# A two-layer network on one core: the feed-forward weights are quantised in five wide pieces between the first tiles' steps

## Chip, cores and metric

One core of a Trainium2 chip runs the whole network in one launch. The metric is the device time in microseconds (us); of several executions the median counts. The engines are named TensorE (PE, with its weight loads PEld), VectorE (DVE), ScalarE (ACT), Pool (GpSimd) and SP, which here only issues DMAs.

## The reference, cut to what matters

The network has two layers over 8 batches of 1024 tokens of width 256: attention and a feed-forward block, then two Mamba layers and a second feed-forward block. Each block's input is normalised and modulated, and its output is scaled by a gate and added to what came in. The change is in the feed-forward block, which is called twice with other weights:

```python
def fp4_quant_dequant(x):
    xb = x.reshape(shape[:-1] + (shape[-1] // 16, 16))
    scale = jnp.maximum(jnp.max(jnp.abs(xb), axis=-1, keepdims=True) / 6.0, 1e-12)
    idx = jnp.searchsorted(_MID, jnp.abs(xb / scale))
    return (_GRID[idx] * jnp.sign(xb / scale) * scale).reshape(shape)

def fp4_linear(x, w):
    return jnp.einsum('bsk,nk->bsn', fp4_quant_dequant(x), fp4_quant_dequant(w))

gate = fp4_linear(x, w_gate)        # w_gate, w_up: 704 x 256, w_down: 256 x 704
h = jax.nn.silu(gate) * fp4_linear(x, w_up)
x = x_in + gb * fp4_linear(h, w_down)      # x is layernorm(x_in) * (1 + cb) + sb
```

Weights and activations are both quantised along their rows, in groups of 16, to a 4-bit grid.

## The kernel before

The phases run one after the other. Each phase is a block of five programs, one for an engine, that hand over by semaphores; between blocks stand two barriers of all engines, with the clearing of the semaphores between them. The two feed-forward calls (`ffn_phase`) are the sixth part and the last part of the program.

In `ffn_phase` the weights come first, in a block of their own, `turn_weights`. It has 14 jobs: six slices of `w_gate` of 128 rows (the last has 64) by 256 columns, six of `w_up`, and two of `w_down` of 128 rows by 704 columns. SP loads a slice, VectorE quantises it in place with ten instructions (`fp4_round`, then `fp4_scale`), TensorE transposes it by chunks of 128 columns (L203), and ScalarE copies each chunk from PSUM into `wg`, `wu` or `wd` (L214). All buffers but the temporary ones are double.

Then a second block works through 64 tiles of 128 tokens. Its five programs are in step by `run`, which calls a `body` for n = -4, -3, ... and in it works on tiles at up to seven stages at once: `early` (statistics of tile n+4, on VectorE and Pool), `ahead` (ScalarE centres tile n+3, L1600; Pool multiplies and adds the modulation, L1414 and L1420), `norm` (quantising the input of tile n+2: VectorE L1469 to L1530, ScalarE L1604, Pool's scale L118), `turn` (tile n+1: TensorE transposes it, ScalarE copies it, TensorE multiplies it by `wg` and `wu`, L1578), `middle` (tile n: VectorE multiplies gate and up, L1476, and quantises the 704 columns of the result; ScalarE L1618, Pool L118), `hturn` and `last` (transposes and product with `wd`, L1548, gate and residual). So the first body that touches a weight is that of n = -1. The order of each engine's queue is that of the code, and an engine that waits for a semaphore runs nothing behind that wait. At the head of the block SP loads the modulation rows (`mod`, the same 24 KB into each of the 128 partitions); VectorE and Pool wait for it before anything else.

Of the kernel before, what the change touches and what calls it, by code (L numbers as in the profile page):

```python
# [10 lines left out]
U32 = mybir.dt.uint32  # L11
# [4 lines left out]
P = 128  # L16
# [1238 lines left out]
def ffn_phase(nc, name, x_in, x_out, mods, w_gate, w_up, w_down, ident, batches):  # L1255
# [7 lines left out]
    with ExitStack() as ctx:  # L1263
        def sb(n, shape, dt=FP32):
            return ctx.enter_context(nc.sbuf_tensor(f"{name}_{n}", shape, dt))
# [10 lines left out]
        wd = sb("wd", [P, FC, D])  # L1276
        jobs = []
        for w, t in ((w_gate, wg), (w_up, wu)):
            for r in range(0, FFN, P):
                n = min(P, FFN - r)  # L1280
                jobs.append((w[r:r + n, :], "fp4", [t[:, c, r:r + n] for c in range(DC)]))
        for r in range(0, D, P):
            jobs.append((w_down[r:r + P, :], "fp4",
                         [wd[0:min(P, FFN - c * P), c, r:r + P] for c in range(FC)]))
        turn_weights(nc, f"{name}_w", ident, jobs)

        mod = sb("mod", [P, batches, 3, D])
        x = sb("x", [P, 2, D])
# [24 lines left out]
        out_ps = pb("out_ps", [P, BANK])  # L1313

        s_mod, s_half = sem("mod_loaded"), sem("half_set")
        s_x = [sem(f"x_loaded{i}") for i in range(2)]
# [9 lines left out]
        s_xstep, s_hstep = sem("xstep_done"), sem("hstep_done")  # L1326
        s_store = [sem(f"stored{i}") for i in range(2)]
        QSTEPS, AT_MASK = 7, 5
        TIGHT = 1.0 + 2.0 ** -22
# [8 lines left out]

        def run(eng, body):


            for n in range(-4, 4):
                body(Tile(n // 2, n % 2), *stages(n))
            with eng.Fori(2, tiles // 2 - 2) as j:
                for u in range(2):
                    body(Tile(j, u), *stages(4))
            for n in range(tiles - 4, tiles + 2):
                body(Tile(n // 2, n % 2), *stages(n))
# [9 lines left out]
        def _(sp):  # L1358
            sp.dma_start(mod[:, :, :, :].rearrange("p b k d -> p b (k d)"), mods.rearrange("b k d -> b (k d)")
                         .unsqueeze(0).to_broadcast([P, batches, 3 * D])).then_inc(s_mod, 16)  # L1360

# [13 lines left out]
            load_x(Tile(0, 1))  # L1375
            load_xr(Tile(0, 0))
            for t in range(2, 6):
                load_x(Tile(t // 2, t % 2))
# [20 lines left out]
        def _(pool):  # L1399
            pool.memset(magic[:, :], MAGIC).then_inc(s_magic, 1)  # L1400
            pool.memset(half[:, :], -0.5).then_inc(s_half, 1)
            pool.memset(eps[:, :], EPS).then_inc(s_half, 1)
            pool.wait_ge(s_mod, 16)
            pool.wait_ge(s_half, 2)

            def body(t, early, ahead, norm, turn, middle, hturn, last):
# [39 lines left out]
                if middle:  # L1446
# [3 lines left out]
                    fp4_scale(pool, hq[:, u, :], hscale[:, :], P, FFN).then_inc(s_hq, 1)  # L1450
            run(pool, body)

        @block.vector
        def _(dve):
            dve.wait_ge(s_mod, 16)
            v = nc.vector

            def blocks(a):
                return a.rearrange("p (n k) -> p n k", k=BLOCK)

            def body(t, early, ahead, norm, turn, middle, hturn, last):
# [69 lines left out]
                if middle:  # L1531
# [3 lines left out]
                    hstep.issued(v.tensor_tensor(hd, hd, htmp[:, :], ALU.subtract))  # L1535
            run(dve, body)

        @block.tensor
        def _(pe):
            def body(t, early, ahead, norm, turn, middle, hturn, last):  # L1540
                if last:
# [28 lines left out]
                if turn:  # L1570
# [4 lines left out]
                    for w, at in ((wg, 0), (wu, 2)):  # L1575
# [5 lines left out]
                        mm.then_inc(s_gate if at == 0 else s_gu, 1)  # L1581
            run(pe, body)

        @block.scalar
        def _(act):
            act.wait_ge(s_magic, 1)

            def body(t, early, ahead, norm, turn, middle, hturn, last):
# [31 lines left out]
                if turn:  # L1620
# [5 lines left out]
                                         gu_ps[:, 0:2, 0:HALF], ACT.Silu).then_inc(s_silu, 1)  # L1626
            run(act, body)

# [765 lines left out]
```

## Time and profile before

| | us |
|---|---|
| median of three executions | 9688.74 |
| the other two | 9687.07, 17838.1 |
| the profiled execution, its own time | 9684.03 |
| its span, first to last instruction | 9682.3 |
| VectorE busy | 8401.1 (87%) |
| TensorE busy, mean granted clock | 8268.4 (85%), 0.939 |
| ScalarE, Pool busy | 5602.5 (58%), 4998.8 (52%) |

All stages and durations below are from the profiled execution, whose span starts at 0. A busy share over the whole program says little here, since it is a mean over phases that have different limits; the stages around the change must be looked at by themselves.

### The profile page before, as it was taken

What the parts mean: (1) busy time and instruction counts of PE and PEld (TensorE: products, weight loads), DVE (VectorE), ACT (ScalarE), POOL (GpSimd) and SP (SyncE); (2) the same over time, 40 slices, a digit from 0 to 9 for tenths busy, and PEclk for the clock granted to TensorE, in tenths of its full rate; (3) what the DMA queues carried; (4) which work ended last, traced back from release to release, by engine and by line L of the source; (5) the groups of instructions that cost most, each with busy time, mean ns of one, the idle gap of its engine ahead of it and who ended that gap; (6) DMA issues with size and microseconds to landing.
All of it is one profiled execution on the core that took longest, in us unless ns stands there. A gap on an engine that the chain in (4) does not pass through costs nothing. (4 is left out here: it accounts for less than half of the span.)

```text
span 9682.3 us, 173958 instructions
## 1 busy us (share of the span) xinstructions
PE 8268.4 (85%) x48396; PEld 4738.3 (49%) x48396; DVE 8401.1 (87%) x13204; ACT 5602.5 (58%) x9153; POOL 4998.8 (52%) x4685
## 2 busy tenths in 40 slices
PE   5679999999999997599688888887688888888599
PEld 2356667666666665366233333333233333333366
DVE  4668888888888886799599999999599999999799
ACT  2257777777777774233466666665466656555233
POOL 0000000000000000388599999999599999999487
PEclk7789999999999998799899999999899999999799
DMA  6789888888888887211112222111122222221111
GB/s 191 252 266 284 278 283 282 282 282 282 282 280 282 280 284 224 71 42 42 72 66 78 80 80 80 72 55 75 63 78 86 89 89 89 89 75 65 46 42 41
DMA packets 1174163, 1447.35 MB, mean 149 GB/s; under 512 B 83658, under 2 KB 1053914, under 8 KB 1140992
## 3 DMA queue, kind: packets, MB, share of 16 engines
q1 hardware_dynamic: 1173824, 1444.18, 45.4%
q14 instruction: 291, 2.38, 0.1%
q8 instruction: 48, 0.79, 0.0%
HBM read 880.81 MB, written 564.60 MB: 149 GB/s over the span
## 5 line engine op out<-in xcount | busy, mean ns | idle before, releaser
L1964 POOL TENSOR_TENSOR mb_bx<-mb_dtu,mb_bc 128x512 f32<-128x512 f32 x2048 | 2665.2, 1325 | 7.7 <-DVE mb_hs L2064 7.4
L2207 PE MATMUL mb_y_ps<-mb_g,ident 128*128 128x512 f32 x4096 | 2189.0, 641 | 467.9 <-DVE mb_g L2024 238.1
L2251 ACT ACTIVATE mb_dA<-mb_dt,mb_a_neg 128x512 f32<-128x512 f32 x2048 | 1403.3, 689 | 1616.2 <-DVE mb_hs L2064 1080.0
L1400 POOL MEMSET f_magic<- 128x1 f32 x2 | 0.2, 99 | 3617.7 <-POOLq L127 3617.7
L2207 PEld LDWEIGHTS mb_y_ps<-mb_g,ident 128*128 128x128 f32 x4096 | 763.6, 199 | 1646.1 <-issue 726.1
L1011 ACT ACTIVATE at_tab<-at_e_ps 128x384 f32<-128x384 f32 x2064 | 1015.1, 492 | 774.9 <-PE at_e_ps L928 773.5
L1065 DVE TENSOR_REDUCE at_nmax<-at_s_ps 128x1 f32<-128x1024 f32 x1025 | 1255.4, 1225 | 35.2
L944 PE MATMUL at_pT_ps<-ident,at_probs 128*128 128x128 f32 x8192 | 1117.7, 279 | 102.5 <-ACT at_probs L1016 81.9
L1016 ACT ACTIVATE at_probs<-at_s_ps,at_nmax 128x1024 f32<-128x1024 f32 x1025 | 1142.9, 1115 | 60.4 <-DVE at_nmax L1065 39.2
L944 PEld LDWEIGHTS at_pT_ps<-ident,at_probs 128*128 128x128 f32 x8192 | 894.3, 141 | 413.2 <-ACT at_probs L1016 384.9
L2024 DVE TENSOR_TENSOR mb_g<-mb_hs,mb_bc 128x512 f32<-128x512 f32 x1472 | 996.1, 677 | 33.8 <-PE mb_y_ps L2207 32.4
L2064 DVE TENSOR_TENSOR_SCAN mb_hs<-mb_dA,mb_carry,mb_bx 128x512 f32<-128x512 f32 x736 | 936.2, 1284 | 97.3 <-POOL mb_bx L1964 36.3
L2064 DVE TENSOR_TENSOR_SCAN mb_hs<-mb_dA,mb_bx 128x512 f32<-128x512 f32 x736 | 896.9, 1224 | 75.1 <-POOL mb_bx L1964 36.9
L911 PE MATMUL at_s_ps<-at_opnd 105*128 105x512 bf16 (+3 forms) x2818 | 805.0, 326 | 7.4 <-DMA at_skew<-at_tables 7.4
L1971 POOL TENSOR_TENSOR mb_g<-mb_hs_sb,mb_bc 128x512 f32<-128x512 f32 x576 | 750.9, 1304 | 88.3 <-PE mb_y_ps L2207 80.1
L1063 DVE TENSOR_TENSOR at_s_ps<-at_s_ps,at_skew 128x384 f32<-128x384 f32 (+1 forms) x1025 | 543.1, 530 | 272.5 <-PE at_s_ps L915 156.0
L1070 DVE COPY at_probsT<-at_pT_ps 128x512 f32<-128x512 f32 x1024 | 697.4, 681 | 0.0
L963 PE MATMUL at_c_ps<-at_probsT,at_val 128*32 128x128 f32 x16384 | 659.7, 279 | 1.6 <-ACT at_probsT L1023 1.6
L915 PE MATMUL at_s_ps<-ident,at_skew 128*128 128x128 f32 x2818 | 609.3, 274 | 0.0
L2140 PE MATMUL mb_ring<-mb_xc,mb_diag 128*128 128x512 f32 x1024 | 522.9, 596 | 48.2 <-ACT mb_u L2304 45.1
L963 PEld LDWEIGHTS at_c_ps<-at_probsT,at_val 128*32 128x32 f32 x16384 | 384.9, 109 | 211.9 <-issue 201.6
L915 PEld LDWEIGHTS at_s_ps<-ident,at_skew 128*128 128x128 f32 x2818 | 392.2, 142 | 85.0 <-issue 0.4
(236 smaller groups left out, 14151.9 us busy)
## 6 DMA issues: line engine op xcount, KB each, us to landing
at_tables<-at_tab SPq DMA_DIRECT2D x1032, 384.0 KB, 3.9
at_skew<-at_tables SPq DMA_DIRECT2D x1030, 256.0 KB, 3.1
mb_bc<-mb_bc_rows SPq DMA_DIRECT2D x256, 1024.0 KB, 6.4
at_skew<-at_tables SPq DMA_DIRECT2D x773, 128.0 KB, 3.5
at_opnd<-at_q_st SPq DMA_DIRECT2D x130, 210.0 KB, 4.4
at_opnd<-at_kl_st SPq DMA_DIRECT2D x130, 210.0 KB, 4.7
at_opnd<-at_kr_st SPq DMA_DIRECT2D x130, 210.0 KB, 4.7
at_q_st<-st_parts SPq DMA_DIRECT2D x96, 256.0 KB, 3.2
```

Source lines behind the costliest of these rows:

```text
L911: mm = nc.tensor.matmul(s_ps[:, b, a * P:z * P], opnd[:, u, 0, q], opnd[:, u, side, a * P:z * P], start=True, stop=(len(near) == 0))
L915: mm = nc.tensor.matmul(s_ps[:, b, kt * P:(kt + 1) * P], skew[:, u, 1, kt, blk * P:(blk + 1) * P], ident[:, :], start=False, stop=(kt == n ...
L944: mm = nc.tensor.transpose(pT_ps[:, hb, k * P:(k + 1) * P], probs[:, i % 2, c:c + P], ident[:, :])
L963: mm = nc.tensor.matmul(c_ps[lane * VW:(lane + 1) * VW, q:q + P], val[:, h.u, k + lane, :], probsT[:, i0 % 2, (k + lane) * P:(k + lane + 1 ...
L1011: nc.scalar.activation(tab[:, e, :], e_ps[:, 0:BAND], ACT.Copy).then_inc(s_tab, 1)
L1016: nc.scalar.activation(probs[:, i % 2, :], s_ps[:, i % 2, :], ACT.Exp, bias=nmax[:, i % 2:i % 2 + 1], scale=1.0).then_inc(s_exp, 1)
L1065: nc.vector.tensor_reduce(nmax[:, b:b + 1], s_ps[:, b, :], axis=AX.X, op=ALU.max, negate=True).then_inc(s_max, 1)
L1964: pool.tensor_tensor(bx[:, s % RINGS, :], dtu[:, c, :], bc[:, 0, n, :], ALU.mult).then_inc(s_bx, 1)
L2024: nc.vector.tensor_tensor(g[:, s1 % RINGS, :], state(s1), bc[:, 1, n, :], ALU.mult).then_inc(s_g, 1)
L2064: nc.vector.tensor_tensor_scan(state(s), dA[:, s % DA_RING, :], bx[:, s % RINGS, :], initial=carry[:, s:s + 1] if k.u else 0.0, op0=ALU.mu ...
L2207: nc.tensor.matmul(y_ps[:, c % 2, :], ident[:, :], g[:, s1 % RINGS, :], start=False, stop=(n == STATE - 1)).then_inc(s_y, 1)
L2251: nc.scalar.activation(dA[:, s % DA_RING, :], dt[:, c, :], ACT.Exp, scale=a_neg[:, c, n:n + 1]).then_inc(s_dA, 1)
```

## The change

The block `turn_weights` is gone from the feed-forward phase. The weights are now cut into five pieces, each a tile of 128 partitions: rows 0 to 127 and 128 to 255 of `w_down` (704 columns each), the first 640 rows of `w_gate` as five slices side by side (1280 columns), the same of `w_up` (1280), and the 64 remaining rows of both, one above the other (256). A function `prepare(k)` of each engine's program does one step: VectorE runs the front half of piece k (absolute maximum, stride, reciprocal, product, mask: five instructions) and the back half of piece k-1 (add, subtract). ScalarE makes the magic number between them, in place of a VectorE instruction, and Pool works out the scale and multiplies by it. TensorE transposes piece k-1 into `gu_ps`, the PSUM tile that holds gate and up later, and ScalarE copies the whole of it to `wg`, `wu` or `wd` in one or two instructions. `run` calls `prepare(0)` and `prepare(1)`, then `prepare(2)`, `(3)`, `(4)` and `(5)` each ahead of the bodies n = -4, -3, -2 and -1. TensorE doesn't start the body n = -1 before all five pieces have been copied. The load of `mod` is issued behind those of the weights and of the first tiles; VectorE waits for it in `prepare(5)`, Pool in `prepare(3)`.

```diff
--- before.py
+++ after.py
@@ -1274,16 +1274,28 @@
         wg = sb("wg", [P, DC, FFN])
         wu = sb("wu", [P, DC, FFN])
         wd = sb("wd", [P, FC, D])
-        jobs = []
-        for w, t in ((w_gate, wg), (w_up, wu)):
-            for r in range(0, FFN, P):
-                n = min(P, FFN - r)
-                jobs.append((w[r:r + n, :], "fp4", [t[:, c, r:r + n] for c in range(DC)]))
-        for r in range(0, D, P):
-            jobs.append((w_down[r:r + P, :], "fp4",
-                         [wd[0:min(P, FFN - c * P), c, r:r + P] for c in range(FC)]))
-        turn_weights(nc, f"{name}_w", ident, jobs)
-
+
+        edge = FFN // P * P
+        tail = FFN - edge
+        widths = (FFN, FFN, edge // P * D, edge // P * D, D)
+        starts = tuple(sum(widths[:k]) for k in range(len(widths)))
+        jobs = len(widths)
+        raw = sb("w_raw", [P, sum(widths)])
+        made = sb("w_made", [P, sum(widths)])
+        wtmp = sb("w_tmp", [P, sum(widths)])
+        wamax, wstride, winv, wscale = (sb(n, [P, sum(widths) // BLOCK]) for n in ("w_amax", "w_stride", "w_inv", "w_scale"))
+
+        def part(a, k):
+            return a[:, starts[k]:starts[k] + widths[k]]
+
+        def blocks_of(a):
+            return a.rearrange("p (n k) -> p n k", k=BLOCK)
+
+        def part_blocks(a, k):
+            return a[:, starts[k] // BLOCK:(starts[k] + widths[k]) // BLOCK]
+
+        def spread(a, k):
+            return part_blocks(a, k).unsqueeze(2).to_broadcast([P, widths[k] // BLOCK, BLOCK])
         mod = sb("mod", [P, batches, 3, D])
         x = sb("x", [P, 2, D])
         xr = sb("xr", [P, 2, D])
@@ -1312,6 +1324,8 @@
         hT_ps = pb("hT_ps", [P, 2 * BANK])
         out_ps = pb("out_ps", [P, BANK])
 
+        turned_up = gu_ps[:, :, :].rearrange("p (c a) w -> p c (a w)", c=DC)
+        turned_down = gu_ps[:, 0:2, :].rearrange("p a w -> p (a w)")
         s_mod, s_half = sem("mod_loaded"), sem("half_set")
         s_x = [sem(f"x_loaded{i}") for i in range(2)]
         s_xr = [sem(f"xr_loaded{i}") for i in range(2)]
@@ -1325,6 +1339,10 @@
         s_shift, s_magic = sem("shift_done"), sem("magic_set")
         s_xstep, s_hstep = sem("xstep_done"), sem("hstep_done")
         s_store = [sem(f"stored{i}") for i in range(2)]
+        s_raw = [sem(f"weights_loaded{k}") for k in range(jobs)]
+        s_wfront, s_wstep, s_wback, s_wscale = sem("wfront"), sem("wstep"), sem("wback"), sem("wscale")
+        s_wq, s_wT, s_wkept = sem("wq"), sem("wT"), sem("w_kept")
+        FRONT, BACK = 5, 2
         QSTEPS, AT_MASK = 7, 5
         TIGHT = 1.0 + 2.0 ** -22
         xt = x_in.rearrange("(n p) d -> n p d", p=P)
@@ -1336,10 +1354,13 @@
 
             return [0 <= n + ahead < tiles for ahead in (4, 3, 2, 1, 0, -1, -2)]
 
-        def run(eng, body):
-
-
+        def run(eng, body, prepare):
+
+            for k in range(2):
+                prepare(k)
             for n in range(-4, 4):
+                if n + 6 <= jobs:
+                    prepare(n + 6)
                 body(Tile(n // 2, n % 2), *stages(n))
             with eng.Fori(2, tiles // 2 - 2) as j:
                 for u in range(2):
@@ -1356,8 +1377,8 @@
 
         @block.sync
         def _(sp):
-            sp.dma_start(mod[:, :, :, :].rearrange("p b k d -> p b (k d)"), mods.rearrange("b k d -> b (k d)")
-                         .unsqueeze(0).to_broadcast([P, batches, 3 * D])).then_inc(s_mod, 16)
+            for k in range(2):
+                sp.dma_start(part(raw, k), w_down[k * P:(k + 1) * P, :]).then_inc(s_raw[k], 16)
 
             def load_x(t):
                 ge(sp, s_centered, t.n - 1)
@@ -1374,6 +1395,13 @@
             load_x(Tile(0, 0))
             load_x(Tile(0, 1))
             load_xr(Tile(0, 0))
+            for k, w in ((2, w_gate), (3, w_up)):
+                sp.dma_start(part(raw, k).rearrange("p (i d) -> p i d", d=D),
+                             w[0:edge, :].rearrange("(i p) d -> p i d", p=P)).then_inc(s_raw[k], 16)
+            for at, w in ((0, w_gate), (tail, w_up)):
+                sp.dma_start(part(raw, 4)[at:at + tail, :], w[edge:FFN, :]).then_inc(s_raw[4], 16)
+            sp.dma_start(mod[:, :, :, :].rearrange("p b k d -> p b (k d)"), mods.rearrange("b k d -> b (k d)")
+                         .unsqueeze(0).to_broadcast([P, batches, 3 * D])).then_inc(s_mod, 16)
             for t in range(2, 6):
                 load_x(Tile(t // 2, t % 2))
 
@@ -1400,8 +1428,20 @@
             pool.memset(magic[:, :], MAGIC).then_inc(s_magic, 1)
             pool.memset(half[:, :], -0.5).then_inc(s_half, 1)
             pool.memset(eps[:, :], EPS).then_inc(s_half, 1)
-            pool.wait_ge(s_mod, 16)
             pool.wait_ge(s_half, 2)
+
+            def prepare(k):
+                if k < jobs:
+                    pool.wait_ge(s_wfront, FRONT * k + 1)
+                    pool.tensor_scalar(part_blocks(wscale, k), part_blocks(wamax, k), 1.0 / 6.0, 1e-12,
+                                       ALU.mult, ALU.max).then_inc(s_wscale, 1)
+                if k > 0:
+                    pool.wait_ge(s_wscale, k)
+                    pool.wait_ge(s_wback, BACK * k)
+                    out = blocks_of(part(made, k - 1))
+                    pool.tensor_tensor(out, out, spread(wscale, k - 1), ALU.mult).then_inc(s_wq, 1)
+                if k == 3:
+                    pool.wait_ge(s_mod, 16)
 
             def body(t, early, ahead, norm, turn, middle, hturn, last):
                 t4, t3, t2, t0 = t.plus(4), t.plus(3), t.plus(2), t.plus(-2)
@@ -1448,12 +1488,31 @@
                     pool.wait_ge(s_hscale, k + 1)
                     pool.wait_ge(s_hchain, (k + 1) * QSTEPS)
                     fp4_scale(pool, hq[:, u, :], hscale[:, :], P, FFN).then_inc(s_hq, 1)
-            run(pool, body)
+            run(pool, body, prepare)
 
         @block.vector
         def _(dve):
-            dve.wait_ge(s_mod, 16)
             v = nc.vector
+
+            def prepare(k):
+                if k < jobs:
+                    front = Steps(dve, s_wfront, FRONT * k)
+                    src, out = part(raw, k), part(made, k)
+                    dve.wait_ge(s_raw[k], 32 if k == 4 else 16)
+                    front(v.tensor_reduce(part_blocks(wamax, k), blocks_of(src), axis=AX.X, op=ALU.max, apply_absolute_value=True))
+                    front(v.tensor_scalar(part_blocks(wstride, k), part_blocks(wamax, k), TIGHT / 6.0, TIGHT * 1e-12,
+                                          ALU.mult, ALU.max))
+                    front(v.reciprocal(part_blocks(winv, k), part_blocks(wstride, k)))
+                    front(v.tensor_tensor(blocks_of(out), blocks_of(src), spread(winv, k), ALU.mult))
+                    front.issued(v.tensor_scalar(part(wtmp, k).bitcast(U32), out.bitcast(U32), STEP_BITS, None, ALU.bitwise_and))
+                if k > 0:
+                    back = Steps(dve, s_wback, BACK * (k - 1))
+                    out, tmp = part(made, k - 1), part(wtmp, k - 1)
+                    dve.wait_ge(s_wstep, k)
+                    back(v.tensor_tensor(out, out, tmp, ALU.add))
+                    back.issued(v.tensor_tensor(out, out, tmp, ALU.subtract))
+                if k == jobs:
+                    dve.wait_ge(s_mod, 16)
 
             def blocks(a):
                 return a.rearrange("p (n k) -> p n k", k=BLOCK)
@@ -1533,10 +1592,33 @@
                     hstep.issued(v.tensor_tensor(hd, hd, htmp[:, :], ALU.add))
                     hstep.wait()
                     hstep.issued(v.tensor_tensor(hd, hd, htmp[:, :], ALU.subtract))
-            run(dve, body)
+            run(dve, body, prepare)
 
         @block.tensor
         def _(pe):
+            def prepare(k):
+                if k == 0:
+                    return
+                m = k - 1
+                w = part(made, m)
+                pe.wait_ge(s_wq, m + 1)
+                ge(pe, s_wkept, m)
+                if m < 2:
+                    for c in range(FC):
+                        cw = min(P, FFN - c * P)
+                        mm = nc.tensor.transpose(turned_down[0:cw, c * P:(c + 1) * P], w[:, c * P:c * P + cw], ident[:, :])
+                elif m < 4:
+                    for i in range(edge // P):
+                        for c in range(DC):
+                            mm = nc.tensor.transpose(turned_up[:, c, i * P:(i + 1) * P],
+                                                     w[:, i * D + c * P:i * D + (c + 1) * P], ident[:, :])
+                else:
+                    for c in range(DC):
+                        mm = nc.tensor.transpose(turned_up[:, c, 0:P], w[:, c * P:(c + 1) * P], ident[:, :])
+                mm.then_inc(s_wT, 1)
+                if k == jobs:
+                    pe.wait_ge(s_wkept, jobs)
+
             def body(t, early, ahead, norm, turn, middle, hturn, last):
                 if last:
                     t0 = t.plus(-2)
@@ -1579,11 +1661,31 @@
                                                       w[:, c, a * HALF:(a + 1) * HALF],
                                                       start=(c == 0), stop=(c == DC - 1))
                         mm.then_inc(s_gate if at == 0 else s_gu, 1)
-            run(pe, body)
+            run(pe, body, prepare)
 
         @block.scalar
         def _(act):
             act.wait_ge(s_magic, 1)
+
+            def prepare(k):
+                if k < jobs:
+                    act.wait_ge(s_wfront, FRONT * (k + 1))
+                    nc.scalar.activation(part(wtmp, k), part(wtmp, k), ACT.Identity, bias=magic[:, :],
+                                         scale=MAGIC_STEP).then_inc(s_wstep, 1)
+                if k == 0:
+                    return
+                m = k - 1
+                act.wait_ge(s_wT, m + 1)
+                if m < 2:
+                    nc.scalar.activation(wd[:, 0:FC - 1, m * P:(m + 1) * P],
+                                         turned_down[:, 0:edge].rearrange("p (c t) -> p c t", t=P), ACT.Copy)
+                    keep = nc.scalar.activation(wd[0:tail, FC - 1, m * P:(m + 1) * P], turned_down[0:tail, edge:edge + P], ACT.Copy)
+                elif m < 4:
+                    keep = nc.scalar.activation((wg if m == 2 else wu)[:, :, 0:edge], turned_up[:, :, 0:edge], ACT.Copy)
+                else:
+                    nc.scalar.activation(wg[:, :, edge:FFN], turned_up[:, :, 0:tail], ACT.Copy)
+                    keep = nc.scalar.activation(wu[:, :, edge:FFN], turned_up[:, :, tail:2 * tail], ACT.Copy)
+                keep.then_inc(s_wkept, 1)
 
             def body(t, early, ahead, norm, turn, middle, hturn, last):
                 if turn:
@@ -1624,7 +1726,7 @@
                     ge(act, s_h, k - 1)
                     nc.scalar.activation(gate[:, u, :].rearrange("p (a w) -> p a w", a=2),
                                          gu_ps[:, 0:2, 0:HALF], ACT.Silu).then_inc(s_silu, 1)
-            run(act, body)
+            run(act, body, prepare)
 
 
 SLOTS = IC * STATE
```

## Rows read from the trace of the kernel before

**Rows 1.** Windows: busy us (instructions) of PE, PEld, DVE, ACT, POOL; clock, DMA share, GB/s.
```profile
3929.50:3991.20 61.70, 10.92 (x36) 5.64 (x36) 51.00 (x140) 7.33 (x36) 0.01 (x1) 0.50 0.12 35
3991.20:4002.40 11.20, 0.00 (x0) 0.00 (x0) 0.00 (x0) 0.00 (x0) 0.15 (x3) 0.50 0.84 317
4002.40:4014.10 11.70, 0.69 (x2) 0.29 (x2) 6.86 (x24) 2.15 (x5) 7.44 (x18) 0.50 0.09 23
4014.10:4616.30 602.20, 566.46 (x2302) 384.33 (x2302) 577.74 (x1192) 232.16 (x445) 489.97 (x685) 0.99 0.13 41
8992.20:9076.30 84.10, 11.61 (x38) 5.93 (x38) 57.97 (x164) 9.45 (x41) 7.61 (x21) 0.50 0.21 71
```

**Rows 2.** Groups by form of VectorE, first weight stage: busy us, mean ns.
```profile
L118 DVE TENSOR_TENSOR f_w_made<-f_w_made,f_w_scale 128x704 f32<-128x704 f32 x2 | 1.8, 892 | 0.1
...
L87 DVE TENSOR_REDUCE f_w_amax<-f_w_raw 128x44 f32<-128x704 f32 x2 | 1.7, 873 | 0.0
...
L103 DVE TENSOR_SCALAR f_w_tmp<-f_w_made 128x704 uint32<-128x704 uint32 x2 | 1.1, 526 | 0.1
L96 DVE RECIPROCAL f_w_inv<-f_w_amax 128x44 f32<-128x44 f32 x2 | 0.9, 428 | 0.1
```

**Rows 3.** Timeline, operands of 1024 columns: start us, duration us.
```profile
8978.49 1.23 DVE L2092 TENSOR_TENSOR mb_o_sb<-mb_o_sb,mb_ln 128x1024 f32<-128x1024 f32 x1
...
8982.31 2.34 POOL L2002 TENSOR_TENSOR mb_o_sb<-mb_o_sb,mb_xin 128x1024 f32<-128x1024 f32 x1 [7.23 <-DVE mb_o_sb L2101]
```

**Rows 4.** DMA issues, 3920 to 4060 us: KB each, median us to landing.
```profile
f_mod<-mods SPq DMA_DIRECT2D x1, 3072.0 KB, 10.8
...
f_w_raw<-w_down SPq DMA_DIRECT2D x2, 352.0 KB, 2.9
...
f_w_raw<-w_up SPq DMA_DIRECT2D x5, 128.0 KB, 2.0
```

**Rows 5.** Groups by form of ScalarE and Pool, 3929 to 4040 us.
```profile
L118 POOL TENSOR_TENSOR f_hq<-f_hq,f_hscale 128x704 f32<-128x704 f32 x2 | 2.8, 1388 | 1.8 <-DVE f_hq L1535 1.8
...
L1618 ACT ACTIVATE f_htmp<-f_htmp,f_magic 128x704 f32<-128x704 f32 x2 | 1.8, 884 | 2.2 <-DVE f_htmp L1520 2.2
...
L1612 ACT ACTIVATE f_hqT<-f_hT_ps 128x640 f32<-128x640 f32 x1 | 0.7, 683 | 0.0
```

**Rows 6.** Timeline, transposes and the last copies of the weight stage.
```profile
3938.88 0.69 PE L203 MATMUL f_w_turned<-ident,f_w_made 128*128 128x128 f32 x2 [2.84 <-DVE f_w_made L118]
...
3987.07 1.54 PE L203 MATMUL f_w_turned<-ident,f_w_made 128*128 128x128 f32 x6 [4.99 <-DVE f_w_made L118]
```

**Rows 7.** Timeline, first tiles of feed-forward block one.
```profile
4004.67 0.60 ACT L1600 ACTIVATE f_xn<-f_x,f_shift,f_rstd 128x256 f32<-128x256 f32 x1 [14.94 <-POOL f_shift L1440]
...
4008.06 0.60 ACT L1600 ACTIVATE f_xn<-f_x,f_shift,f_rstd 128x256 f32<-128x256 f32 x1 [2.79 <-POOL f_shift L1440]
4008.33 0.29 DVE L1499 TENSOR_SCALAR f_xtmp<-f_xq 128x256 uint32<-128x256 uint32 x1
...
4012.27 0.61 POOL L118 TENSOR_TENSOR f_xq<-f_xq,f_xscale 128x256 f32<-128x256 f32 x1
4012.30 0.74 DVE L1499 TENSOR_SCALAR f_xtmp<-f_xq 128x256 uint32<-128x256 uint32 x1
...
4014.10 5.00 PE L1578 MATMUL f_gu_ps<-f_wg,f_xqT 128*128 128x352 f32 x8 [0.47 <-ACT f_xqT L1594]
...
4021.51 0.89 DVE L1476 TENSOR_TENSOR f_h<-f_gate,f_gu_ps 128x704 f32<-128x704 f32 x1 [4.31 <-PE f_gu_ps L1578]
```

**Rows 8.** Timeline, product of gate and up, two tiles apart, late in block two.
```profile
9304.62 0.88 DVE L1476 TENSOR_TENSOR f_h<-f_gate,f_gu_ps 128x704 f32<-128x704 f32 x1
...
9323.06 0.88 DVE L1476 TENSOR_TENSOR f_h<-f_gate,f_gu_ps 128x704 f32<-128x704 f32 x1
```

**Rows 9.** The same instruction early in block two, one tile apart.
```profile
9119.74 0.88 DVE L1476 TENSOR_TENSOR f_h<-f_gate,f_gu_ps 128x704 f32<-128x704 f32 x1
...
9129.70 0.88 DVE L1476 TENSOR_TENSOR f_h<-f_gate,f_gu_ps 128x704 f32<-128x704 f32 x1
```

## The prediction

> **What bounds the kernel now.** I first cut the span by stage, with the windows view, since only two short stretches are touched. From the first weight load of block one to its first product of the input with the weights, 84.6 us pass in three parts [rows 1]. In the first (61.7 us) VectorE is busy for 51.0, every other engine for 11 or less: 14 slices go through ten dependent instructions each, and the rest is waits and hand-offs. In the second (11.2 us) nothing computes; the 3 MB of modulation are on their way at 317 GB/s, and VectorE and Pool wait for them. In the third (11.7 us) the first two tiles go through statistics, centring and quantising with no engine near full. Block two repeats it: 84.1 us [rows 1]. Behind each stands a loop over 64 tiles in which VectorE is busy for 577.7 of 602.2 us [rows 1]. The change can shorten the 168.7 us of the two openings; the tile loops are the same code. So 1.7% of the time is all that is at stake, unless the loops are disturbed.
>
> About 2% is also what a measurement of this kernel can tell from no change; the forecast lies inside it.
>
> **Prices of wide instructions.** VectorE's fp32 product takes 0.89 us at 704 columns and 1.23 at 1024 [rows 2, 3], 1.06 ns a column, so 1.50 at 1280 and 0.42 at 256. The reduction (0.87 at 704) grows alike, to 1.48; the mask (0.53) runs at half that price, to 0.83; the reciprocal (0.43 for 44 groups) goes to 0.7 for 80 [rows 2]. With 0.2 us for the stride and five hand-offs of 0.03, a front half costs 3.1 us at 704 columns, 4.9 at 1280, 1.7 at 256; a back half 1.85, 3.05, 0.9. Sum over the five pieces: 17.7 + 10.7 = 28.4 us of VectorE in place of 51.0, by fewer fixed parts, one instruction dropped (the doubled scale) and three passes given away (magic number, scale, its multiply).
> Pool's multiply by the scale takes 0.61 at 256 and 1.39 at 704 [rows 7, 5]; at 1280 it was never run. Its own slope gives 2.4; the plain 128x1024 operation (2.34 [rows 3]) would give 2.9. I take 2.4, the same form. ScalarE's magic number: 0.88 at 704 [rows 5], under 1.6 at 1280; it stands under VectorE's front of the next piece and costs nothing, and if that cover went it would cost some 1.3 us a piece. ScalarE's copy out of PSUM: 0.68 for 640 columns [rows 5], so 1.2 for 1280 (at most 1.37, twice the row). TensorE's transposes at granted clock 0.50: 0.69 us for two, 1.54 for six [rows 6, 1], so 2.4 for ten.
>
> **The loads.** Ahead of `mod` SP now issues 2.5 MB. A 352 KB slice lands 2.9 us after its issue, a lone 128 KB one 2.0, and the 3072 KB of `mod` 10.8 [rows 4]. Streams this deep are nearest to `mod`: at its 285 KB/us `w_gate` lands at about 8 us and `mod` at 21.5, against a need at 11 and 33. At the lone slice's 64 KB/us `mod` would land at 87; that end goes to the rivals.
>
> **The new opening, walked in the order of the queues** (us from the first load's issue). VectorE begins at 3.0. Fronts 0 to 3 (16.0), backs 0 to 2 (6.8) and the statistics of tile 0 (0.7) bring it to 26.6. Up to here nothing else delays it. Then the queues bind: `prepare(3)` stands ahead of the body that centres tile 0, so ScalarE can't centre before it has copied piece 2 (`w_gate`). That copy comes after Pool's multiply (to 29.0) and ten transposes (31.5), and ends at 32.7. VectorE ends front 4 and back 3 at 32.2 and then waits for tile 0. From centring tile 0 to the end of its mask the trace has 3.95 us (4004.67 to 4008.62) [rows 7], which brings us to 36.7. In the same time Pool does tile 0's modulation and tile 1's statistics, which stand ahead of its multiply of piece 3. So piece 3 goes the same way: Pool 36.6 to 39.0, transposes 41.4, copy 42.6, and only then is tile 1 centred. From that to Pool's last scale of tile 0 the trace has 4.2 us (4008.06 to 4012.27) [rows 7]: 46.9. Pool scales tile 0, then piece 4 (0.61 each, to 48.1); back 4 of VectorE fits ahead of that. Two transposes (0.7) and two short copies (0.5) make the last weights ready at 49.4, and tile 0's own transpose and copy (1.1) give the first product at 50.5.
> To that I add 1.4 us for Pool and VectorE in each other's way. The row: VectorE's mask of 256 columns takes 0.29 us alone and 0.74 beside Pool's multiply, ending just behind it [rows 7]. The multiply of piece 2 (26.6 to 29.0) meets VectorE's stride of piece 4 at 27.9, which makes 1.1, and that of piece 4 makes 0.3. First product: 51.9.
> Against 84.6 and 84.1 this saves 32.7 and 32.2, in all 65 us. From the first product to the product of gate and up (7.4 us, [rows 7]) and in the loop behind it nothing is edited, so no time is moved there. The barriers between the two old blocks (1.4 us) are within the 84.6.
> The profiled execution took 9684.0 us; less 65, 9619. The median of the runs is 4.7 us above it, so 9624.
>
> **Rivals.**
> *VectorE alone decides.* If the hand-offs through ScalarE and Pool overlapped better than walked, what is left is VectorE's work, 3.0 + 28.4 + 4.6 for tiles 0 to 2 in between, and a tail of 3.3 us: first product at 39.3. That gives 45 a block, 9599. Against it: the centring of tile 0 can't pass the copy in ScalarE's queue.
> *Full lock.* If every wide Pool multiply held VectorE for its whole length (1.4 + 1.4 + 2.4 + 2.4 + 0.6 = 8.2 us) on the path, the first product would come at 58.7: 26 a block, 9638. Against it: the multiplies begin when VectorE turns to reductions and statistics, and in the row on Pool's 704-column multiply (1388 ns mean) no time shows in which it was held itself [rows 5].
> The Trainium skill (SBUF — State Buffer, Who interferes with whom) states this as a rule: an operation with two SBUF inputs or in a two-port mode and a Pool operation that reads SBUF exclude each other for the whole instruction, while a reduction never takes part. The stretched mask agrees with it; whether it bites for 8 us or for 1.4 is decided by the order in the queues.
> *Late loads.* With the 1 KB rows of `w_gate` and `w_up` at a rate between the two bounds, say 130 KB/us, `w_gate` would land at 15 and `mod` at 44: 11 us lost a block, 9646. Below 85 KB/us the opening would be no shorter than now.
> *The other side: the tile loop falls into another rhythm.* VectorE and Pool grant each other turns by who comes first, so the tiles' spacing depends on how they begin. Late in block two two tiles take 18.44 us [rows 8], 9.22 each; early there is one of 9.96 [rows 9]. The new opening hands the loop other starting times. If every tile stayed at 9.96, 128 x 0.74 = 95 us would be lost: 9719, slower than before. It decides from 0.51 us a tile on (65/128). Against it: both blocks come from slightly different openings and the long spacings don't last.
> *It doesn't do what it says:* the pieces go through, but the first tiles' steps only follow them, with no gain from the overlap: first product at 49.4 + 11.7 = 61.1, 23 a block, 9643.
>
> **How the numbers follow.** The forecast, 9624, gets 0.68; VectorE alone (9599) 0.08; full lock (9638) 0.11; late loads (9646) 0.04; no overlap (9643) 0.05; the loop's rhythm (9719) 0.04. The uncertain prices are Pool's wide multiply (0.5 us twice on the path), the stall (0 to 8) and the transposes. The range 9592 to 9658 takes in all but the slower rival and a little of the edges. By the 2% bound (9495 and 9883): faster 0.01, same 0.97, slower 0.02.
>
> **What would show it.** Right: one stage of about 52 us from the first `w_down` load to the first product; VectorE idle for 2 to 3 us before tile 0's reduction, with the centring behind the copy of `w_gate`; `mod` landed well ahead of Pool's wait; two tiles in 18.4 us later on. Wrong: VectorE waiting for a weight load after the first; Pool's 1280-column multiply at 3 us or more; stretched VectorE instructions all through the opening; or a spacing above 9.5 us a tile in the middle of the loops.

## The result and the profile after

The changed kernel takes 9621.76 us (median of five, 9612.91 to 9630.83) against 9688.74 before; the ratio, from the means of the runs, is 0.9934, 95% interval 0.9920 to 0.9948. By the 2% bound that is the same time, as forecast, but the interval leaves no doubt that it is shorter. Forecast were 9624 and a range of 9592 to 9658. One run of the kernel before took 17838.1 us; it is left out of the ratio.

A whole-program difference of 67 us is small beside what unedited stages vary by, so the two profiled executions are first laid side by side by stage. Each boundary is the first DMA issue or the first product of its stage.

| stage (us) | before | after | difference |
|---|---|---|---|
| start to the first weight load of block one | 3929.5 | 3939.8 | +10.3 |
| opening of block one, to the first product with `wg` | 84.6 | 50.1 | -34.5 |
| from there to the next phase's first load | 608.0 | 607.8 | -0.2 |
| on to the first weight load of block two (Mamba) | 4370.0 | 4374.1 | +4.0 |
| opening of block two | 84.2 | 49.8 | -34.4 |
| from there to the end | 606.0 | 607.6 | +1.6 |
| span | 9682.3 | 9629.1 | -53.2 |

The openings give 68.9 us; 65 were forecast. The unedited stages take 15.7 back in this pair of executions. In the eight profiles of changed kernels that are told of here the first stage lies between 3931.9 and 3943.8 us, in the two of the kernel before and of a variant of it at 3929.5 and 3926.6. The medians differ by 67.0 and, in a second comparison, 67.5 us (the means by 63.6 and 65.9), close to what the openings alone give; but the intervals reach from some 50 to 78 us, so a loss of 10 is unlikely and not excluded. Where a changed kernel was run five times (after, c1, e6), the profiled execution was the slowest of the five, 9 to 11.5 us above the median. What makes the first stage longer in these executions stays open.

The windows view of after, with the columns of [rows 1]: the opening of block one in three parts, the loop behind it, and the opening of block two.

```profile
3939.80:3942.90 3.10, 0.00 (x0) 0.00 (x0) 0.00 (x0) 0.00 (x0) 0.17 (x3) 0.50 0.67 209
3942.90:3966.50 23.60, 3.08 (x12) 2.18 (x12) 22.82 (x34) 6.20 (x8) 6.56 (x11) 0.50 0.59 214
3966.50:3989.88 23.38, 6.17 (x24) 4.57 (x24) 12.52 (x26) 5.12 (x10) 11.50 (x18) 0.50 0.04 12
3989.88:4592.10 602.22, 565.49 (x2302) 384.00 (x2302) 577.17 (x1192) 231.13 (x445) 491.54 (x686) 0.99 0.13 41
8971.75:9021.53 49.78, 9.26 (x37) 6.76 (x37) 35.34 (x59) 11.33 (x18) 18.22 (x31) 0.50 0.35 120
```

The 84.6 us of before were 61.7 of weights, 11.2 of waiting for the modulation and 11.7 of first tiles [rows 1]. Now 3.1 us pass until the first piece has landed, then VectorE is busy for 22.82 of 23.60 us, and then for only 12.52 of 23.38. So the opening has two halves of another kind: one that VectorE's work sets, and one in which no engine is busy for much more than half (VectorE for 54%, Pool for 49). In all VectorE works 35.3 us in it, where before it was 51.0 + 6.9 [rows 1]. The loop stage reads as before: 577.2 of 602.2 us.

The second half in the timeline of after (start, duration; in brackets the idle time ahead of it and what ended that):

```profile
3963.87 1.49 DVE L1513 TENSOR_TENSOR f_w_made<-f_w_made,f_w_tmp 128x1280 f32<-128x1280 f32 x1
...
3965.51 2.37 POOL L1442 TENSOR_TENSOR f_w_made<-f_w_made,f_w_scale 128x1280 f32<-128x1280 f32 x1 [5.04 <-DVE f_w_made L1513]
...
3966.26 1.65 DVE L1503 TENSOR_SCALAR f_w_stride<-f_w_amax 128x16 f32<-128x16 f32 x1
...
3967.94 2.40 PE L1613 MATMUL f_gu_ps<-ident,f_w_made 128*128 128x128 f32 x10 [7.71 <-POOL f_w_made L1442]
...
3970.37 1.24 ACT L1684 ACTIVATE f_wg<-f_gu_ps 128x1280 f32<-128x1280 f32 x1 [6.53 <-PE f_gu_ps L1613]
...
3971.50 0.59 ACT L1702 ACTIVATE f_xn<-f_x,f_shift,f_rstd 128x256 f32<-128x256 f32 x1
...
3973.79 0.42 DVE L1528 TENSOR_REDUCE f_xamax<-f_xn 128x16 f32<-128x256 f32 x1 [1.88 <-POOL f_xn L1460]
...
3975.71 2.37 POOL L1442 TENSOR_TENSOR f_w_made<-f_w_made,f_w_scale 128x1280 f32<-128x1280 f32 x1
...
3980.57 1.24 ACT L1684 ACTIVATE f_wu<-f_gu_ps 128x1280 f32<-128x1280 f32 x1 [8.08 <-PE f_gu_ps L1613]
3981.70 0.59 ACT L1702 ACTIVATE f_xn<-f_x,f_shift,f_rstd 128x256 f32<-128x256 f32 x1
...
3982.72 0.72 DVE L1587 TENSOR_TENSOR f_xq<-f_xq,f_xtmp 128x256 f32<-128x256 f32 x1 [6.67 <-ACT f_xtmp L1706]
...
3986.06 0.62 POOL L118 TENSOR_TENSOR f_xq<-f_xq,f_xscale 128x256 f32<-128x256 f32 x1
...
3989.88 5.06 PE L1660 MATMUL f_gu_ps<-f_wg,f_xqT 128*128 128x352 f32 x8 [0.47 <-ACT f_xqT L1696]
```

Read it as a relay. VectorE ends back 2 (3963.87 + 1.49, and passes on at 3965.5). Pool multiplies for 2.37, TensorE transposes for 2.40, ScalarE copies for 1.24, and only then, at 3971.50, is tile 0 centred, as ScalarE's queue has it. VectorE had by then been through with all it could do and was idle for 1.88 us ahead of tile 0's reduction (3973.79). The second lap (Pool 3975.71, copy 3980.57, centring of tile 1 3981.70) is worse: VectorE is idle for 6.67 us ahead of tile 0's addition (3982.72), which waits for ScalarE's step for tile 0, in the queue behind the copy and tile 1's centring. One row shows how VectorE and Pool exclude each other: the stride instruction of piece 4, 16 values, lasts 1.65 us and ends at 3967.91, 0.03 behind Pool's multiply. It holds hardly anything up, since VectorE has to wait for tile 0 anyway.

The DMA issues of after, KB each and median us to landing:

```profile
f_mod<-mods SPq DMA_DIRECT2D x1, 3072.0 KB, 12.8
f_w_raw<-w_down SPq DMA_DIRECT2D x2, 352.0 KB, 3.3
f_w_raw<-w_gate SPq DMA_DIRECT2D x1, 640.0 KB, 5.1
```

The modulation, issued at 3944.4 behind 2.5 MB of other loads, lands some 17 to 18 us into the opening; Pool first uses it at 32, once tile 0 is centred. Against [rows 4] `w_down` and `mod` take a little longer, and none is waited for but the first.

Two tiles of the loop late in block two, to be set beside [rows 8]:

```profile
9304.72 0.88 DVE L1535 TENSOR_TENSOR f_h<-f_gate,f_gu_ps 128x704 f32<-128x704 f32 x1
...
9323.15 0.88 DVE L1535 TENSOR_TENSOR f_h<-f_gate,f_gu_ps 128x704 f32<-128x704 f32 x1
```

18.43 us for two tiles, 18.44 before: the loop has fallen into the same rhythm.

### The profile page after: what moved, and what is told of

The parts are those of the page before. It is cut to its first block and busy times, and to the rows that moved or that the text cites. A ratio compares the mean times of both kernels' runs of the same rounds, so it can differ in the third digit from the quotient of the medians.

```text
span 9629.1 us, 173618 instructions
## 1 busy us (share of the span) xinstructions
PE 8271.7 (86%) x48392; PEld 4744.6 (49%) x48392; DVE 8357.6 (87%) x12994; ACT 5596.0 (58%) x9107; POOL 5015.8 (52%) x4705
## 3 DMA queue, kind: packets, MB, share of 16 engines
q14 instruction: 289, 2.37, 0.1%
## 5 line engine op out<-in xcount | busy, mean ns | idle before, releaser
L2073 POOL TENSOR_TENSOR mb_g<-mb_hs_sb,mb_bc 128x512 f32<-128x512 f32 x576 | 750.8, 1304 | 93.1 <-PE mb_y_ps L2309 84.2
```

## The experiments

Times are the opening of block one and of block two, from the profile; a total is given where several runs were made. Before: 84.6, 84.2. After: 50.1, 49.8, and once more with the experiments (c1) 50.1, 50.0. Single runs gave totals of 9617.99 (e1), 9613.67 (e2), 9627.91 (e3), 9633.35 (e4) and 9633.92 us (e7); they are too few to weigh, and the openings are read instead.

### c1: the changed kernel again

> The changed kernel once more, on the same chip as the others: openings of 50 us, ratio to the kernel before 0.993.

Openings 50.14 and 49.97 us; 9617.66 us (median of five) against 9685.13, ratio 0.9932 (0.9919 to 0.9946). The openings repeat within 0.2 us, so effects of 1 us are read from them, not from totals. Loops won't do for that: from first product to the end of its stage they take 603.9 to 608.4 us in the ten profiles, with the same code in nearly all.

### e1: all pieces ahead of the first tiles

```diff
-            for k in range(2):
+            for k in range(jobs + 1):
                 prepare(k)
             for n in range(-4, 4):
-                if n + 6 <= jobs:
-                    prepare(n + 6)
                 body(Tile(n // 2, n % 2), *stages(n))
```

> All six steps of the weights stand ahead of the first body, so that nothing of a tile runs between them. The opening (first load's issue to first product) is 50.1 and 49.8 us in the changed kernel. Theory A (the order in the queues of ScalarE and Pool sets the opening): the five pieces run through without a stop, the last is copied at about 36 us, and the first tiles' 11.7 us stand behind it: 47.5 us, 3 less than with the steps between. Rival B (the overlap with the first tiles is where the gain comes from): the 11.7 us are added to weights that end at 49: 56 to 61 us.

Openings 48.48 and 48.52 us: 1.4 shorter without any overlap. Rival B falls: putting the weights between the tiles' steps, in this order, is not where the gain comes from, it costs a little. Theory A had 47.5, but by two errors that partly cancel: the last piece is copied at 39.1 us, not 36, and what follows takes 9.4, not 11.7. The first is mostly two short instructions of VectorE that Pool's wide multiplies hold back, the stride of piece 4 (2.18 us) and this one (timeline of e1):

```profile
3968.13 2.63 POOL L1440 TENSOR_TENSOR f_w_made<-f_w_made,f_w_scale 128x1280 f32<-128x1280 f32 x1 [3.83 <-DVE f_w_made L1511]
3968.56 2.47 DVE L1511 TENSOR_TENSOR f_w_made<-f_w_made,f_w_tmp 128x256 f32<-128x256 f32 x1
...
3975.65 0.60 ACT L1700 ACTIVATE f_xn<-f_x,f_shift,f_rstd 128x256 f32<-128x256 f32 x1
...
3977.88 0.42 DVE L1526 TENSOR_REDUCE f_xamax<-f_xn 128x16 f32<-128x256 f32 x1 [4.49 <-POOL f_xn L1458]
```

The subtraction of piece 4 (0.42 us alone) takes 2.47 and ends 0.27 behind Pool's multiply of piece 3. VectorE then has 4.49 us of nothing ahead of tile 0's reduction: the first tiles run alone.

### e2: ScalarE centres before it copies

```diff
                                          scale=rstd[:, 1:2]).then_inc(s_centered, 1)
+                if isinstance(t.j, int) and t.n == -3:
+                    keep_piece(2)
...
                                          scale=MAGIC_STEP).then_inc(s_xstep, 1)
+                if isinstance(t.j, int) and t.n == -2:
+                    keep_piece(3)
```

`keep_piece(m)` is the copying part of ScalarE's `prepare`, which in turn leaves these two out.

> Only ScalarE's order is changed: the copies of pieces 2 and 3 out of PSUM stand behind the centring of tiles 0 and 1, not ahead of it. Theory A (queue order): tile 0 is centred while Pool still scales piece 2, and tile 1 while Pool scales piece 3; VectorE has no gap ahead of tile 0's reduction; opening 42 us, 8 less. Rival C (VectorE's work sets the opening): no instruction is taken away, so it stays at 50 us. Rival D (VectorE and Pool exclude each other): Pool's multiplies meet more of VectorE's two-operand work than before, and half or more of the 8 us is lost again: 46 us or more.

Openings 43.78 and 43.59 us. That is 6.3 shorter with the same instructions on every engine, so the order of one queue makes up that much of the opening, and rival C falls. Theory A had 42: 1.7 of the 8 are missing. Rival D's mechanism is seen, but for a fifth of the gain, not half; that it accounts for all of the 1.7 is not shown. The timeline of e2:

```profile
3960.09 0.58 ACT L1703 ACTIVATE f_xn<-f_x,f_shift,f_rstd 128x256 f32<-128x256 f32 x1
...
3967.36 1.49 DVE L1513 TENSOR_TENSOR f_w_made<-f_w_made,f_w_tmp 128x1280 f32<-128x1280 f32 x1
3967.39 1.91 POOL L1478 TENSOR_TENSOR f_rstd<-f_rstd,f_half 128x1 f32<-128x1 f32 x1
...
3968.76 0.41 DVE L1528 TENSOR_REDUCE f_xamax<-f_xn 128x16 f32<-128x256 f32 x1
...
3970.01 2.37 POOL L1442 TENSOR_TENSOR f_w_made<-f_w_made,f_w_scale 128x1280 f32<-128x1280 f32 x1
3970.17 2.36 DVE L1558 TENSOR_SCALAR f_xtmp<-f_xq 128x256 uint32<-128x256 uint32 x1
...
3979.97 5.03 PE L1660 MATMUL f_gu_ps<-f_wg,f_xqT 128*128 128x352 f32 x8 [0.47 <-ACT f_xqT L1697]
```

Tile 0 is centred at 3960.09, 23.9 us into the opening (31.7 in after); VectorE goes on to tile 0's reduction (3968.76) with no gap. Now the engines get in each other's way in both directions: Pool's one-column power takes 1.91 us in place of 0.58, beside VectorE's subtraction of 1280 columns, and tile 1's centring waits for the result; VectorE's mask takes 2.36 in place of 0.29, beside Pool's multiply.

### e3: the scale's multiply on VectorE

```diff
-                if k > 0:
-                    pool.wait_ge(s_wscale, k)
-                    pool.wait_ge(s_wback, BACK * k)
-                    out = blocks_of(part(made, k - 1))
-                    pool.tensor_tensor(out, out, spread(wscale, k - 1), ALU.mult).then_inc(s_wq, 1)
...
-                    back.issued(v.tensor_tensor(out, out, tmp, ALU.subtract))
+                    back(v.tensor_tensor(out, out, tmp, ALU.subtract))
+                    dve.wait_ge(s_wscale, k)
+                    v.tensor_tensor(blocks_of(out), blocks_of(out), spread(wscale, k - 1), ALU.mult).then_inc(s_wq, 1)
```

> The five multiplies by the scale go from Pool (0.6 to 2.4 us each) to VectorE (0.4 to 1.5 us each), 5.8 us more of VectorE and 8.2 less of Pool. Theory A (queue order): the way of pieces 2 and 3 to TensorE is 0.9 us shorter each and Pool is free for tile 0: opening 46 to 47 us. Rival C (VectorE's work sets it): 5.8 us longer, 56 us. Rival D (VectorE held by Pool's wide multiplies): the stretched stride instruction of 1.65 us goes, and no other change is seen beside the 5.8.

Openings 46.05 and 45.81 us: 4.0 shorter, with five multiplies more for the busiest engine (0.42 to 1.89 us each, 5.6 in all). Rival C would have been 10 longer than that. In the timeline of e3 the multiply of piece 2 takes 1.49 in place of Pool's 2.37, and the stride is back at 0.17:

```profile
3971.18 1.49 DVE L1510 TENSOR_TENSOR f_w_made<-f_w_made,f_w_scale 128x1280 f32<-128x1280 f32 x1
...
3972.72 2.40 PE L1610 MATMUL f_gu_ps<-ident,f_w_made 128*128 128x128 f32 x10 [8.14 <-DVE f_w_made L1510]
...
3973.56 0.17 DVE L1498 TENSOR_SCALAR f_w_stride<-f_w_amax 128x16 f32<-128x16 f32 x1
...
3976.29 0.59 ACT L1699 ACTIVATE f_xn<-f_x,f_shift,f_rstd 128x256 f32<-128x256 f32 x1
...
3977.77 1.89 DVE L1510 TENSOR_TENSOR f_w_made<-f_w_made,f_w_scale 128x1280 f32<-128x1280 f32 x1
...
3983.28 0.59 ACT L1699 ACTIVATE f_xn<-f_x,f_shift,f_rstd 128x256 f32<-128x256 f32 x1
```

So the share that went to Pool was no gain. But the shorter multiply is the smaller part of it. Tile 0 is centred 32.5 us into the opening (3976.29), 0.8 later than in after. From there to tile 1's centring e3 takes 7.0 us and after 10.2, since VectorE multiplies piece 3 at once (3977.77), where in after that multiply stood in Pool's queue behind tile 0's modulation and tile 1's statistics (3975.71, 4.2 us behind the centring). From tile 1's centring to the first product it is 6.5 against 8.2. Pool's order counts here as ScalarE's does in e2.

### e4: the modulation first

The one edit is that the load of `mod` is issued ahead of the first weight load.

> The 3 MB of modulation are issued ahead of the weights, as in the kernel before, and nothing else is changed. Theory A: the transfers share one set of engines in order, so the first piece of weights lands 8 to 11 us later and the opening grows by as much, to 58 to 61 us; what the moved load is worth is then about 10 us a block. Rival E (the load is hidden anyway, since 352 KB find room beside it): opening within 2 us of 50.

Openings 58.20 and 58.31 us, 8.1 and 8.5 longer. VectorE's first reduction starts 11.3 us after the first issue, not 3.1, in both blocks, which is the whole difference but for 0.3 us. Rival E falls. The timeline of e4:

```profile
3936.31 4.19 SPq L1401 DMA_DIRECT2D f_w_raw<-w_up  x1
...
3943.28 0.89 DVE L1502 TENSOR_REDUCE f_w_amax<-f_w_raw 128x44 f32<-128x704 f32 x1 [17.19 <-DMA f_w_raw<-w_down]
```

The first row is SP's issue of `w_up`, which took 4.19 us while the 3 MB were on their way, and 0.53 in after (4.37 in block two of e4).

### e5: the kernel before, with the modulation loaded early

```diff
-        turn_weights(nc, f"{name}_w", ident, jobs)
+        turn_weights(nc, f"{name}_w", ident, jobs, load_mod)
```

SP's program in `turn_weights` calls `load_mod` behind its last weight load; the load at the head of the second block is gone.

> The kernel before, with one edit: the load of the modulation is issued behind the last weight load of the weight block, 16 us ahead of that block's end. Theory A: the load is hidden under VectorE's work, and what then stands between the blocks is the load of the first tile, 2.3 us after its issue: opening 75 to 76 us in place of 84.6 and 84.1, in all 17 us less than before. Rival G (the barriers or the first tile's load take the place of the wait): under 4 us less a block.

Openings 77.21 and 75.28 us, 7.4 and 8.9 shorter; 9666.27 us (median of ten) against 9685.13, ratio 0.9981 (0.9972 to 0.9990). Rival G falls. What is left between the blocks is the first tile's load, 4.0 us from its issue to VectorE's first statistics in block one and 2.2 in block two; why it is slower in block one stays open. The timeline of e5 has the load under the weights, 16.8 us ahead of the second block's first issue:

```profile
3971.31 0.44 SPq L1291 DMA_DIRECT2D f_mod<-mods  x1
...
3988.12 0.82 SPq L1368 DMA_DIRECT2D f_x<-x  x2
...
4003.82 5.06 PE L1582 MATMUL f_gu_ps<-f_wg,f_xqT 128*128 128x352 f32 x8 [0.47 <-ACT f_xqT L1598]
```

### e6: `w_down` last, and only three pieces ahead of the first product

```diff
-        widths = (FFN, FFN, edge // P * D, edge // P * D, D)
+        widths = (edge // P * D, edge // P * D, D, FFN, FFN)
...
-        turned_down = gu_ps[:, 0:2, :].rearrange("p a w -> p (a w)")
+        turned_down = hT_ps
...
-                if n + 6 <= jobs:
-                    prepare(n + 6)
+                if n < -1 or n == 0:
+                    prepare(n + 6 if n < 0 else jobs)
...
+                if isinstance(t.j, int) and t.n in (-1, 1):
+                    pe.wait_ge(s_wkept, 3 if t.n < 0 else jobs)
```

ScalarE copies behind the centring, as in e2, and SP loads the pieces in their new order; both are left out of the lines above.

> On top of ScalarE's new order (e2) the pieces are taken in another order: w_gate, w_up, their rest, and the two of w_down last, whose transposes go into the PSUM tile of the first tiles' results, which is free until then. The first product waits for three pieces, not five. Theory A (the chain of hand-offs that stands ahead of the first product decides): VectorE's work ahead of it is shorter by the 10 us of the two w_down pieces, of which the chain through Pool, transposes and copies gives back some: opening 39 to 41 us against 43.7, and product to product the tiles then run on unchanged; about 10 us less than e2's openings or 18 to 20 less than the changed kernel in all (0.2%). Rival C (VectorE's total work decides, wherever it stands): the opening is shorter, but the first product of gate and up, or the second, comes as much later, and the time is that of e2.

Openings 41.51 and 41.60 us, 8.6 and 8.4 shorter than c1's; 9598.22 us (median of five) against 9617.66 of c1 and 9685.13 of before, ratio to before 0.9913 (0.9899 to 0.9926). It is the fastest of all: its interval overlaps that of c1 (0.9919 to 0.9946) at the edge, but the slowest of its five runs (9609.02) beats c1's fastest (9611.71), and the openings differ by more than 8 us each. Against e2 the gain is 2.3 and 2.0 us an opening, less than the 2.7 to 4.7 expected. The timeline of e6 shows the last piece's work behind the first product (3983.67), where VectorE was idle for 4.50 us in after:

```profile
3983.67 4.39 PE L1660 MATMUL f_gu_ps<-f_wg,f_xqT 128*128 128x352 f32 x8 [0.47 <-ACT f_xqT L1698]
...
3986.49 0.88 DVE L1512 TENSOR_TENSOR f_w_made<-f_w_made,f_w_tmp 128x704 f32<-128x704 f32 x1
...
3989.52 1.39 POOL L1442 TENSOR_TENSOR f_w_made<-f_w_made,f_w_scale 128x704 f32<-128x704 f32 x1
```

Rival C holds in part: of the 2.3 us gained at the first product in block one 2.2 are left at the third tile's product of gate and up (66.1 us against 68.3), but in block two 1.3 (67.3 against 68.6).

### e7: the magic number on VectorE

```diff
+                    v.tensor_scalar(part(wtmp, k), part(wtmp, k), MAGIC_STEP, MAGIC, ALU.mult, ALU.add).then_inc(s_wstep, 1)
```

with ScalarE's instruction left out.

> The magic number of each piece is made by VectorE, as in the kernel before, not by ScalarE: 0.5 us at 704 columns, 0.8 at 1280, 3.0 in all. Theory A: those of pieces 0 to 3 (2.7 us) stand ahead of back 2, from which the chain through Pool starts, and the last one under a wait: opening 52.5 to 53 us. Rival F (the hand-offs to ScalarE cost as much as they save): 50 us as now.

Openings 52.96 and 52.66 us, 2.9 longer, as theory A had it; rival F falls. What ScalarE took over is a gain by the length of the instructions, as it stands under VectorE's next front.

## Why the prediction was right

**The bounds and the stages.** Right. The edit moved the two openings by 68.9 us; the loops differ by -0.2 and +1.6, within what they vary by among the profiles.

**VectorE's prices.** Fronts 0 to 3 and backs 0 to 2 with tile 0's statistics were to end at 26.6 us; the trace has 25.5 (3965.36 less 3939.82). The extrapolated widths hold within 0.02 us for a product of 1280 columns (1.49, forecast 1.50), a reduction (1.48) and a mask (0.83); the reciprocal took 0.65 and not 0.7. Neighbouring instructions overlap a little more than the 0.03 of hand-off I gave them. Pool's multiply, which I took at 2.4 by its own slope and not at 2.9, was 2.37; ten transposes 2.40 (2.4); the copy 1.24 (1.2).

**The queues.** Right, and shown: the walk gave ScalarE's order as what makes the second half, and e2 takes 6.3 us out by that order alone. The rival by which VectorE alone decides (39.3 us) is refuted by e2 and e3, in which the opening gets shorter with as much or more of VectorE's work.

**The stall of 1.4 us.** The place was right, the effect not: the stride of piece 4 is held until Pool's multiply has ended, 1.65 us against 0.2, but behind it VectorE waits for tile 0 in any case. So the 1.1 us added to the path for it were not there; of the 0.3 for the multiply of piece 4, 0.2 are seen (0.80 in place of 0.61). Without the whole term the walk gives 50.5, and the trace 50.1 and 49.8. It is the largest part of the 1.95 us a block by which I was off. The other part is the start of the relay, 1.1 us earlier than walked, of which some 0.5 arrives at the end. VectorE's idle time ahead of tile 0's reduction was 1.88 us, just short of the 2 to 3 named. The full-lock rival (58.7) falls for the opening as it is; e1 and e2 show the same exclusion where other work meets, and there the openings are 1.0 and 1.7 us above the walk.
The rule in the Trainium skill (SBUF — State Buffer, Who interferes with whom), that an operation of VectorE with two SBUF inputs and one of Pool that reads SBUF exclude each other for a whole instruction, is borne out in both directions: 2.47 us for VectorE's subtraction of 256 columns, which ended 0.27 behind Pool's multiply (e1), and 1.91 for Pool's power, which ended 0.45 behind VectorE's subtraction (e2). VectorE's stride and mask, with one input each, were held in the same way (1.65 us in after, 2.36 in e2).

**The loads.** Right: `w_gate` landed at 7.4 us (8 was the estimate), and `mod` at 17 to 18, where 21.5 was the estimate. e4 and e5 price what hiding it gives by two ways: 8.1 to 8.5 and 7.4 to 8.9 us a block, less than the 11.2 of idle time in [rows 1], since another load stands in its place: the first weights' 3.1 us in after, the first tile's 4.0 and 2.2 in e5.

**"With no gain from the overlap."** I gave this case 61.1 us and 0.05. That the overlap gives no gain in this order is what happened, and the price was wrong: I added the first tiles' 11.7 to weights that were themselves held up by the steps between. With all pieces first it is 48.5 (e1).

**Where the 34.5 us of an opening come from.** Hiding the modulation gives 8 (e4, e5). Magic number on ScalarE: 2.9 (e7). Scale on Pool: a loss of 4.0 (e3), more by its place in Pool's queue than by its length. The steps between: a loss of 1.4 (e1). What remains, some 29 us, is the difference, taking the parts to add up, and not measured by itself: wider instructions, one fewer a piece, the start of the first tiles' loads and the missing barriers. The windows bound one part: VectorE is busy 22.5 us less in the opening (57.9 to 35.3), and 3.0 of magic number and 5.6 of multiplies went to other engines, which leaves some 14 for wider and fewer instructions and the working out of the scale, now Pool's. No run has the wide pieces alone.

**The median.** 9624 against 9621.76: the openings gave 3.9 us more than forecast, and the rest of the median 2 less. That the two figures lie 2.2 us apart is luck, since the interval of the ratio is some 14 us to either side; the account rests on the openings. The prediction's remark that a measurement can tell 2% from no change was far too wide: 0.14% to either side is what these runs give.

## What to carry to other kernels

When steps of two jobs share in-order queues, walk one job's chain through each queue it passes and ask what of the other job stands ahead: ScalarE's four instructions in another order were worth 6.3 us an opening. With the old order the interleaving cost 1.4 us against one job after the other (e1, 48.5); with the new one it gains 4.7 (e2, 43.8). An engine that is mostly idle isn't free if it lies on the chain: the scale's multiply on Pool cost 4.0 us, although Pool was busy for 18 of 50 us, for it waited there behind steps of the tiles. And measure a change to a short stage in that stage: the openings of after repeated within 0.2 us, whole runs of one kernel within 22.

## What the runs showed of the hardware

SP's issue of the `w_up` load took 4.19 and 4.37 us behind a 3 MB transfer (e4), and 0.53 ahead of it (after). Pool's one-column power, 0.58 us alone, took 1.91 beside a 1280-column instruction of VectorE (e2). VectorE's stride of 16 values, 0.17 us alone, took 1.65 (after) and 2.18 us (e1) beside Pool's 1280-column multiply, and ended 0.03 behind it both times.
